# First batch of the first attention: one group's operand stacks built by a selection matmul instead of through memory, with the start-up reordered around it

## What is computed

```
q = l2norm((ln(x) @ Wq.T) per head);  k = l2norm((ln(x) @ Wk.T) per head);  v = (ln(x) @ Wv.T)
attn = softmax(g_scale * q @ k.T)
x = x + attn @ v
```

## Time and profile before

| | us |
|---|---|
| median of 3 runs | 1400.16 (1398.45 to 1401.77) |
| profiled execution: time | 1399.79 |
| profiled execution: span of the trace | 1398.1 |
| PE busy | 1214.7 (87%) |
| DVE busy | 949.8 (68%) |
| ACT busy | 865.9 (62%) |
| POOL busy | 511.7 (37%) |

### The profile page before, as it was taken

One profiled execution on the slowest core, in us unless ns is written; L12 is line 12 of the kernel. 1 busy time (PEld: TensorE's weight loads), 2 busy tenths in 40 slices (PEclk: granted clock), 3 DMA queues, 4 the chain that ended last, 5 costly groups with the idle time before them and its releaser, 6 DMA issues. The chain is left out here.

```text
span 1398.1 us, 22687 instructions
## 1 busy us (share of the span) xinstructions
PE 1214.7 (87%) x6739; PEld 621.9 (44%) x6739; DVE 949.8 (68%) x2869; ACT 865.9 (62%) x1716; POOL 511.7 (37%) x788
## 2 busy tenths in 40 slices
PE   3689999995787899999999999999999999987492
PEld 2233333332462344544544544544545545545272
DVE  5457777755014787888888788888888798784110
ACT  1699999993233667567667566666667567661040
POOL 1100333335371333233434433433434434434255
PEclk9999999997897999999999999999999999999697
DMA  5575444369731666576666666676676666568122
GB/s 145 125 237 170 138 133 131 127 215 217 152 35 39 151 148 154 133 167 152 148 167 149 150 159 153 147 162 151 136 163 151 137 159 144 129 159 233 47 24 23
DMA packets 132937, 197.92 MB, mean 142 GB/s; under 512 B 35166, under 2 KB 76077, under 8 KB 132816
## 3 DMA queue, kind: packets, MB, share of 16 engines
q1 hardware_dynamic: 104848, 138.67, 38.8%
q0 software_dynamic: 27392, 56.76, 19.4%
q10 hardware_dynamic: 576, 1.05, 0.2%
HBM read 61.75 MB, written 39.24 MB: 72 GB/s over the span
## 5 line engine op out<-in xcount | busy, mean ns | idle before, releaser
L1745 ACT ACTIVATE tile<-tile,low 128x512 f32<-128x512 f32 x512 | 363.6, 714 | 246.4 <-DVE low L1831 246.2
L1521 POOL DMA_DIRECT2D crossed<-blocks x512 | 253.8, 504 | 488.9 <-DVE blocks L1844 446.7
L1831 DVE CUSTOM_DVE_ANT_0 tile<-s_ps,bias 128x512 f32<-128x512 f32 x512 | 330.8, 682 | 44.1 <-PE s_ps L1608 37.7
L680 ACT ACTIVATE probs_a<-score_ps,gbound 128x1024 f32<-128x1024 f32 x256 | 264.1, 1132 | 36.5 <-PE score_ps L997 32.1
L1608 PE MATMUL s_ps<-kT,qT 64*128 64x512 f32 x1024 | 261.8, 623 | 15.5 <-DVE low L1831 14.0
L1844 DVE STREAM_TRANSPOSE blocks<-tile 128x512 f32<-128x512 f32 x384 | 256.8, 694 | 0.0
L1628 PE MATMUL o_psb<-crossed,v_b 128*64 128x512 f32 x512 | 238.0, 607 | 15.4 <-DMA crossed<-blocks 13.5
L389 POOL DMA_INDIRECT slots<-rows_r,slot_r x128 | 128.0, 1000 | 72.5 <-issue 49.9
L1608 PEld LDWEIGHTS s_ps<-kT,qT 64*128 64x128 f32 x1024 | 85.7, 186 | 135.1 <-issue 92.1
L1010 PE MATMUL o_ps<-probs_a,v_ext 128*32 128x512 f32 x1024 | 136.0, 604 | 3.3 <-DVE o_sb L805 3.3
L1633 PE MATMUL o_psb<-crossed,v_b 128*64 128x256 f32 x512 | 128.4, 393 | 1.1 <-issue 1.1
(11 more groups left out here) (195 smaller groups left out, 1605.0 us busy)
## 6 DMA issues: line engine op xcount, KB each, us to landing
crossed<-blocks SPq DMA_DIRECT2D x512, 96.0 KB
crossed<-blocks POOLq DMA_DIRECT2D x512, 96.0 KB
inv_row<-inv_rows SPq DMA_DIRECT2D x128, 128.0 KB
q_parts<-parts SPq DMA_DIRECT2D x32, 256.0 KB, 3.0
k_stack<-k_parts SPq DMA_DIRECT2D x32, 256.0 KB, 2.6
q_stack<-q_parts SPq DMA_DIRECT2D x32, 256.0 KB, 3.0
w_f<-in_w SPq DMA_DIRECT2D x32, 256.0 KB, 6.2
k_parts<-parts SPq DMA_DIRECT2D x28, 256.0 KB, 3.9
```

What stands on the lines that cost most here:

```text
L680: nc.scalar.activation(probs[q % 2][:, c % 4 // 2, pair:pair + 2, :].rearrange("p h t -> p (h t)"), score_ps[(b * NCH + c) % 3][:, :], ACT ...
L1521: pool.dma_start(strip_to(n, a, m), strip_from(n, a, m)).then_inc(crossed_sw[n % 2], 16)
L1745: nc.scalar.activation(tile[(b * NS + k) % RING][s][:, :], tile[(b * NS + k) % RING][s][:, :], ACT.Exp, bias=low[n % 2][:, s, i:i + 1], sc ...
L1831: nc.vector.tensor_tensor_reduce(out=tile[(b * NS + k) % RING][s][:, :], in0=s_ps[k % 2][s][:, :], in1=bias[:, h, off:off + S], scale=1.0, ...
```

## The change

- **Selection matmul.** A new constant input `sel` (32 x 4 x 128 ones and zeros) is loaded. After `turn_qk(0, 1)` PE multiplies it with the first 32 rows of `parts`: two matmuls make `q_stack` of group 0, two `k_stack`, into the halves of `score_ps[2]`. DVE copies the q half, ACT the k half. The first batch's group 0 is not read back from memory; groups 1 to 3 still are, and all eight writes to memory stay.
- **Second batch alone.** The load of `x` is split into tiles 4 to 7 and 8 to 31. `statistics(TB, 2 * TB, 2)` stands between the two `take_qk` of batch 0, `prepare(1, 0)` behind the second, and the statistics of the 24 other tiles behind DVE's copy of `q_stack`. POOL has three powers instead of two.
- **Identity matmuls.** One `keep_busy` ahead of the weight transposes, one ahead of `turn_x(0)`, three between `bias_table` and `turn_qk(0, 0)`.

```diff
 # SP
             sp.dma_start(onehot[:, :], g["onehot"]).then_inc(table_in, 16)
-            sp.dma_start(x_res[:, TB:NT, :], x_all[:, TB:NT, :]).then_inc(x_rest, 16)
+            sp.dma_start(sel[:, :, :], g["sel"]).then_inc(sel_in, 16)
+            sp.dma_start(x_res[:, TB:2 * TB, :], x_all[:, TB:2 * TB, :]).then_inc(x_second, 16)
+            sp.dma_start(x_res[:, 2 * TB:NT, :], x_all[:, 2 * TB:NT, :]).then_inc(x_rest, 16)
...
                 for grp in range(GROUPS):
-                    for stack, dram in ((k_stack, k_dram), (q_stack, q_dram)):
+                    for stack, dram in ((k_stack, k_dram), (q_stack, q_dram)) if b >= 1 or grp >= 1 else ():
 # POOL
             inverse_std(0, TB, 1)
             r.constants(pool)
+            inverse_std(TB, 2 * TB, 2)
             wait(pool, v_staged, 0, 1)
             for grp in range(GROUPS):
                 move_v(grp)
-            inverse_std(TB, NT, 2)
+            inverse_std(2 * TB, NT, 3)
 # ACT
             first_k_parts()
+            act.wait_ge(first_ps, 2)
+            nc.scalar.activation(k_stack[0][:, 0, :], score_ps[2][:, S:2 * S], ACT.Copy).then_inc(first_in, 1)
             attend(0, False, True)
 # DVE
             take_qk(0, 0)
+            dve.wait_ge(x_second, 16)
+            statistics(TB, 2 * TB, 2)
             take_qk(0, 1)
+            prepare(1, 0)
             prepare(0, 2)
...
             split(0, 1)
+            dve.wait_ge(first_ps, 1)
+            nc.vector.tensor_copy(q_stack[0][:, 0, :], score_ps[2][:, 0:S]).then_inc(first_in, 1)
             dve.wait_ge(x_rest, 16)
-            statistics(TB, NT, 2)
+            statistics(2 * TB, NT, 3)
             dve.wait_ge(r.const, 4)
-            dve.wait_ge(ln_rstd, 2)
-            prepare(1, 0)
 # PE
             pe.wait_ge(g["consts_ready"], 1)
+            keep_busy(nc, g, o_ps[:, :], 1)
             pe.wait_ge(w_in, 48)
...
                 if first % 8 == 0:
-                    wait(pe, stacks_in[grp], b, 16 * 2)
+                    if b == 0 and grp == 0:
+                        pe.wait_ge(first_in, 2)
+                    else:
+                        wait(pe, stacks_in[grp], b - (grp == 0), 16 * 2)
...
+            keep_busy(nc, g, o_ps[:, :], 1)
             turn_x(0)
             make_qk(0, 0)
             make_qk(0, 1)
             make_v(0)
             bias_table()
+            keep_busy(nc, g, score_ps[0][:, 0:S], 3)
             turn_qk(0, 0)
             turn_qk(0, 1)
+            pe.wait_ge(sel_in, 16)
+            for n in range(2):
+                wait(pe, rest_ready, 0, n + 1)
+                for own in range(2):
+                    last = nc.tensor.matmul(score_ps[2][:, n * S:(n + 1) * S], sel[:, 2 * n + own, :],
+                                            parts[0:32, own, n, :].bitcast(F32), start=(own == 0), stop=(own == 1))
+                last.then_inc(first_ps, 1)
             attend(0, False, True)
```

More of the change, by code:

```diff
@@ L450, in attention_a @@
         w_in, w_ps, w_ready = sem("wa_in"), sem("wa_ps"), sem("wa_ready")
-        x_first, x_rest, e_in, const_step = sem("x_first"), sem("x_rest"), sem("e_in"), sem("const_step")
+        x_first, x_second, x_rest, e_in, const_step = (sem(n) for n in ("x_first", "x_second", "x_rest", "e_in", "const_step"))
         zero_ready = sem("zero_ready")
@@ L455, in attention_a @@
         gs_in, gs_step = sem("gs_in"), sem("gs_step")
+        sel = sb("sel", [32, 4, P])
+        sel_in, first_ps, first_in = sem("sel_in"), sem("first_ps"), sem("first_in")
         clear_a = sem("clear_a")
@@ L551, in batch @@
                 for grp in range(GROUPS):
-                    wait(sp, stacks_in[grp], b, 16 * 2)
-                    sp.sem_inc(g["passed_sp"], 1)
+                    if b >= 1 or grp >= 1:
+                        wait(sp, stacks_in[grp], b - (grp == 0), 16 * 2)
+                        sp.sem_inc(g["passed_sp"], 1)
                 if before:
@@ L728, in prepare @@
                     wait(dve, xT_ps, 0, b)
+                    dve.wait_ge(ln_rstd, min(b, 2) + 1)
                     for i in range(TB):
@@ L2027, in bucket_onehot, with stack_rows @@
     return (np.arange(BUCKETS)[:, None] == bucket[None, :]).astype(np.float32)
+def stack_rows():
+    sel = np.zeros((32, 4, P), np.float32)
+    for row in range(P):
+        h, m, n, d = row // 32, row % 32 // 16, row % 16 // DA, row % DA
+        sel[h * DA + d, n, row] = 1.0
+        sel[h * DA + d, 2 + m, row] = 1.0
+    return sel
 _INS = {"x": "L0_attn_a_x", "a_Wq": "L0_attn_a_Wq", "a_Wk": "L0_attn_a_Wk", "a_Wv": "L0_attn_a_Wv",
@@ L2050 @@
     g["onehot"] = nc.dram_tensor("in_onehot", (BUCKETS, REL), F32, kind="ExternalInput").ap()
+    arrays["in_sel"] = stack_rows()
+    g["sel"] = nc.dram_tensor("in_sel", (32, 4, P), F32, kind="ExternalInput").ap()
     g["out"] = nc.dram_tensor("out_0", (B, S, D), F32, kind="ExternalOutput").ap()
```

## The result

The changed kernel took 1381.92 us (median of 3 runs, 1379.18 to 1385.98) against 1400.16: ratio 0.9873, 95% interval 0.983 to 0.9917, so 12 to 24 us less where 6.1 was forecast. The profiled execution is the one of 1381.92, span 1380.2.

What follows compares the result with a forecast made beforehand. ACT bounds attention a, so the mark was its seventh exponential, delayed by stalls at the start. -4.3 - 2.1 + 0.3 = -6.1 us there, carried to the end: 1393.7 against 1399.8 us; range 1388.8 to 1397.6.

Steps and rivals of the forecast that it cites:

- Gaps for the second batch's statistics and `xn_a`: nothing.: Up to the unit vectors (24.6), DVE's two 2.17 us gaps hide this work; without them it would cost 2.6 us.
- Three identity matmuls: 0.6 late.: On PE from 21.07, ahead of the transposes of q: 0.6 us late, between nothing and 1.7.
- Transposes: 0.7 saved.: Transposes of q and k on PE: at the high clock each set saves 0.45; 0.7 us taken.
- Selections: 5.5.: Four selection matmuls on PE: 7.2 us at low clock, 3.8 at high, the middle 5.5 taken, done at 33.8.
- ACT's copy 0.60 with a free ACT.: After the selections, ACT copies 128x512 from PSUM in 0.60 us; with hand-overs the stack is there at 34.5.
- First exponential -4.3: ACT's first exponential comes at 35.2, 4.3 us earlier.
- new stall -2.1: ACT stalls 2.5 us before the fifth exponential, behind DVE's 24-tile statistics; first to fifth takes 6.8 instead of 8.92, 2.1 less.
- fifth to seventh +0.3: ACT from the fifth to the seventh exponential: 3.4 us instead of 3.08, 0.3 more.
- Memory path: Group 1's stacks read back through memory still decide, landing near 50: no change, 1399 to 1400 us; chance 0.07.
- late tiles: The second batch's tiles load late and hold up DVE: slower if they land after 19.3, up to 1403 us; chance 0.05.
- All later waits are between engines, so the shift goes through to the end.: Behind the seventh exponential: the 6.1 us gained there carries through to the kernel's end, giving 1393.7 us.
- rival 1: PE at the high clock all the way from about 21 us: 9.6 to 11 us less, 1388.5 to 1390.2; chance 0.23.

Runs made afterwards that it cites:

- after_again: The changed kernel, unaltered, measured again: 1385.57 us (6 runs) against 1396.35 for the kernel before, ratio 0.9922.
- only_selection: The kernel before with the selection matmuls only: 0.9985 of the kernel before's time.
- only_identity: The kernel before with the five identity matmuls only, `sel` loaded and unused: 0.9986 of the kernel before's time.
- no_second: The changed kernel with the second batch's statistics, load and power back among 28 tiles, without the wait in `prepare`: 0.9983 of the kernel before's time.
- late_start: The changed kernel with ACT's copy of `k_stack` waiting for 36 memsets on POOL: 0.994 of the kernel before's time.
- more_waits_2: The kernel before with one more DVE wait in each batch's preparation, second group of runs: 0.9964 of the kernel before's time.

## Why the prediction was right or wrong

- *Gaps for the second batch's statistics and `xn_a`: nothing.* Right: no wait at 12.63, `v_stage` at 17.74 against 17.59, the 0.15 coming with the second identity matmul.
- *Three identity matmuls: 0.6 late.* 0.7, with the 0.15 from above 0.9. Counting the 5.8 us of the earlier trace rows from 21.07 gives a rise at 26.9, not the 25 to 26 that were taken; in eight traces the identity matmuls' records shorten between about 24 and 26. *Transposes: 0.7 saved.* 1.0. *Selections: 5.5.* 4.17 in the first trace, 3.7 to 4.6 in four others and 6.9 and 7.2 in two: both ends occur, and the middle that was taken does not.
- *ACT's copy 0.60 with a free ACT.* Its length was right, but with selections this short it was held by ACT itself, which issued the last write of k until 32.94.
- *First exponential -4.3, new stall -2.1, fifth to seventh +0.3.* -5.0, -2.4, +1.4, sum -6.0. The last was mis-sized for this execution: `make_qk(1, 1)` and the first values ran at low throughout (4.45 from the fifth to the seventh; 3.03 in after_again, where they were partly at high). That the sum came within 0.1 is in part luck: the first exponential came 0.7 better than forecast and the stall 0.3, and this stretch 1.1 worse.
- *Memory path and late tiles (rivals 3 and 4).* Neither: nothing waited for `x_second` or for group 1.
- **"All later waits are between engines, so the shift goes through to the end."** This step failed, in two ways. First, what lies behind the mark is not the same from one execution to the next. It differs by 9 us in one kernel (1333.7 and 1343.1 us from the first square behind the mark to the end), and three runs of each met high ones before and low ones after; repeated, the gain is 10.9 (7 to 15). The start's 6.0 became 5.3 by the end of attention a's exponentials in the first pair of traces, which looks like a shift that goes through, but in the second pair 6.4 became 2.7. Second, the change had a part that I gave no term at all, as if a wait that is nearly always fulfilled cost nothing: DVE's wait in every batch's preparation. By itself it took 3.8 and 5.0 us off (between 0.3 and 8.1 by the intervals), about the difference of 10.9 to 6. That is the best supported account of the rest, and not a shown one: only_selection has no such wait and is 5.3 less than its mark gives, only_identity and no_second are 4.0 and 3.1 (no_second's interval reaches 0).
- *The range* took the scatter as half a microsecond; the interval of three runs against three was 12 us wide. The 18.2 of the outset lies outside every rival; the repeated 10.9 is at rival 1's end (9.6 to 11), but its mechanism, high all the way, was seen in no trace.

What stays open is whether the fulfilled wait is the cause, and how it would save time. The traces show six batches of attention b in 621.5 to 624.1 for ten of the eleven traces with such a wait added (625.2 for late_start), and in 624.9 to 626.6 for all nine without. There the value matmuls wait less for the crossing DMAs (7.0 us in the first trace before, 5.3 in the changed kernel's, 3.8 in more_waits_2's); but the wait stands in attention a. A shift of DVE's code by these instructions is a guess that no run tested. Nor was it tried whether it works in another place.

## What to carry to other kernels

Follow a start-up edit to the instruction from which the bound engine runs without gaps, and compare that mark: in the two kernels traced twice it repeated within 0.7 and 1.1 us, where single whole times scatter by ten. It tells what the edit did to the start, and not what arrives at the end. Moving one engine's work earlier is worth only what the next late thing allows: the selection made the first exponential earlier, and at the mark was worth nothing without the second batch's part, nothing with it alone (47.1 against 46.9), and 3.3 with the identity matmuls as well. The second batch's part alone was 9.3 less (6 to 12), which is not told from the whole change's 10.9, so try each part of a change alone before keeping all of it. List every line of the diff that runs in every iteration, a fulfilled wait too, and repeat both kernels before explaining a difference larger than the stretch that was changed.

## What the runs showed of the hardware that was not expected

- With one more wait on DVE per batch, fulfilled when DVE comes to it for nearly all of them, the kernel before took 0.9973 (0.9948 to 0.9998) and 0.9964 (0.9942 to 0.9987) of its time. That the wait is the cause is likely and not shown.
- The same identity matmuls leave PE at high or at low from one execution to the next: the selections behind them took 4.17, 3.85, 3.69, 4.26, 4.62, 6.91 and 7.19 us, and in the last one PE was already at high by 10.00 and at low behind a gap of 3.52.
- Median times of the unaltered kernel before in five groups of runs: 1392.1 to 1396.4, and 1400.2 in the first.
